# Local attention with an overlapped gated MLP: scores ahead of the feed-forward phases, and exponentials ahead of the GELUs, in the gate steps

## The reference, cut to what matters

```python
for i in range(6):
    x = attn_layer(shift_tokens(x), Wqkv[i], q_scale[i], k_scale[i], Wo[i]) + x
    x = ffn_layer(shift_tokens(x), ln_g[i], ln_b[i], W1[i], b1[i], W2[i], b2[i]) + x
# attn_layer: 16 heads of 64; q and k normalised and rotated; windows of 32 queries see
# 64 keys (their own window and the one before): softmax(8 q k + mask) v, then Wo
# ffn_layer:  layer norm, then (a + b1a) * gelu(gate + b1g) @ W2 + b2, inner width 341
```

## The kernel before, in words

| s mod 4 | phases in the step | length of a step |
|---|---|---|
| 0 | 2 | 15.7 us on the mean |
| 1 (gate step) | 3 | 21.0 us on the mean |
| 2 | 4 and 0 | 19.1 us on the mean |
| 3 | 5 and 1 | 18.6 us on the mean |

## Time and profile before

### The profile page before, as it was taken

One profiled execution on the slowest core, in us unless ns is written; L12 is line 12 of the kernel. 1 busy time (PEld: TensorE's weight loads), 2 busy tenths in 40 slices (PEclk: granted clock), 3 DMA queues, 4 the chain that ended last, 5 costly groups with the idle time before them and its releaser, 6 DMA issues. The chain is left out here.

```text
span 4666.0 us, 101858 instructions
## 1 busy us (share of the span) xinstructions
PE 3974.8 (85%) x41249; PEld 2095.7 (45%) x41249; DVE 2827.2 (61%) x5103; ACT 2272.8 (49%) x4209; POOL 1358.8 (29%) x645
## 2 busy tenths in 40 slices
PE   5666977889994997399999999999999969998888
PEld 2223433233332343166666666666666642333335
DVE  4774333676673333587777878787787746672225
ACT  2111212677772332176666666667666624652112
POOL 2441000111100000166666666566665500000000
PEclk8887978799996998699999999999999978997889
DMA  0000000666651000123232232322322200000000
GB/s 15 0 0 19 0 11 13 221 202 195 200 191 43 0 0 3 42 69 91 62 90 59 61 91 59 89 64 57 92 59 60 57 17 1 1 1 10 10 10 10
DMA packets 157210, 265.27 MB, mean 57 GB/s; under 512 B 33940, under 2 KB 69075, under 8 KB 154304
## 3 DMA queue, kind: packets, MB, share of 16 engines
q1 hardware_dynamic: 154674, 258.31, 18.8%
q10 hardware_dynamic: 2062, 0.38, 0.0%
HBM read 89.88 MB, written 68.16 MB: 34 GB/s over the span
## 5 line engine op out<-in xcount | busy, mean ns | idle before, releaser
L1987 POOL TENSOR_TENSOR b2f_norm<-b2f_norm,b2f_minus_half 128x16 f32<-128x16 f32 x192 | 554.8, 2907 | 275.8 <-DVE b2f_norm L2330 275.8
L1977 POOL TENSOR_TENSOR b2f_q<-b2f_q,b2f_q_part 128x1024 f32<-128x1024 f32 x96 | 228.0, 2375 | 951.8 <-DVE b2f_q_part L2320 951.8
L1435 ACT ACTIVATE b1a_weights<-b1a_b_ps 128x512 f32<-128x512 f32 x512 | 277.4, 597 | 41.0 <-PE b1a_b_ps L1358 39.3
L1542 DVE TENSOR_REDUCE b1a_tops<-b1a_a_ps 128x1 f32<-128x512 f32 (+3 forms) x512 | 244.6, 501 | 44.9 <-PE b1a_a_ps L1314 43.3
L1521 DVE TENSOR_REDUCE b3a_tops<-b3a_a_ps 128x1 f32<-128x512 f32 (+3 forms) x384 | 194.5, 552 | 107.2 <-PE b3a_a_ps L1314 104.4
L2329 DVE TENSOR_REDUCE b2f_norm<-xn 128x16 f32<-128x1024 f32 x192 | 234.2, 1220 | 11.9 <-ACT xn L2212 4.8
L2221 ACT ACTIVATE b2f_prob<-b2f_odd_ps,b2f_bias,b2f_norm 128x64 f32<-128x64 f32 x768 | 232.0, 446 | 10.9 <-DVE b2f_bias L2346 10.0
L2221 ACT ACTIVATE b2f_prob<-b2f_even_ps,b2f_bias,b2f_norm 128x64 f32<-128x64 f32 x768 | 231.9, 450 | 2.3 <-DVE b2f_bias L2346 2.3
L1247 POOL TENSOR_SCALAR b1a_k_op<-b1a_k_op,b1a_extra 128x1024 bf16<-128x1024 bf16 x32 | 90.6, 2843 | 485.8 <-ACT b1a_k_op L1456 485.8
L2271 ACT ACTIVATE b2f_v_rows<-b2f_q_ps 128x1024 f32<-128x1024 f32 x96 | 98.2, 1023 | 268.5 <-PE b2f_q_ps L2049 147.3
L1980 POOL TENSOR_TENSOR b2f_k<-b2f_k,b2f_k_part 128x1024 f32<-128x1024 f32 x96 | 227.5, 2370 | 0.8 <-DVE b2f_k_part L2320 0.8
(11 more groups left out here) (498 smaller groups left out, 8940.4 us busy)
## 6 DMA issues: line engine op xcount, KB each, us to landing
b2f_values<-b2f_v_rows SPq DMA_DIRECT2D x1534, 64.0 KB
position_scratch<-b1a_e_sb SPq DMA_DIRECT2D x128, 512.0 KB, 3.0
b1a_band<-position_scratch SPq DMA_DIRECT2D x128, 384.0 KB, 3.9
b2f_wqkv<-in_b2f_wqkv SPq DMA_DIRECT2D x6, 1536.0 KB, 6.5
b2f_turn<-in_c_rotary SPq DMA_DIRECT2D x6, 1024.0 KB, 8.2
b2f_wo<-in_b2f_wo SPq DMA_DIRECT2D x6, 512.0 KB, 9.4
b1f_up<-in_b1f_up SPq DMA_DIRECT2D x1, 2304.0 KB
b1f_down<-in_b1f_down SPq DMA_DIRECT2D x1, 2304.0 KB
```

What stands on the lines that cost most here:

```text
L1435: act.activation(weights[:, s % P_RING, c, lo:QW], b_room(s, c)[:, lo:QW], ACT.Exp).then_inc(S.exps_ready, 1)
L1542: ins = dve.tensor_reduce(out, src, AX_X, ALU.max)
L1977: pool.tensor_tensor(G.q[:, g % 2], G.q[:, g % 2], G.q_part[:], ALU.add) \
L1987: pool.tensor_tensor(part, part, G.minus_half[:, 0:HEADS], ALU.pow) \
```

## The change

In gate steps TensorE does the scores ahead of project_v and the phases, as in all other steps; and ScalarE does the 16 exponentials ahead of the GELUs. No wait, no buffer and no instruction of the two engines is added or removed by the source; the semaphores' waits stay inside the functions that move.

```diff
@@ tensor, step loop
-                gates = any(phase == 3 for f, phase in feed_forward(s))
-                if not gates and 0 <= s - 1 < n_tiles:
+                if 0 <= s - 1 < n_tiles:
                     scores(s - 1, here)
                 if s < n_tiles:
                     project_v(s)
                 feed(s, range(6))
-                if gates and 0 <= s - 1 < n_tiles:
-                    scores(s - 1, here)
                 if 0 <= s - 2 < n_tiles:
                     weigh_values(s - 2, other)
@@ scalar, step loop
-                ffn(s, 3)
                 if 0 <= s - 1 < n_tiles:
                     exps(s - 1, here)
+                ffn(s, 3)
                 ffn(s, 0)
```

## The result

The changed kernel takes 4741.59 us (median of 4 runs, 4739.1 to 4745.72) against 4668.3 us for the kernel before, measured beside it (4 runs). The ratio is 1.0155, with a 95% interval of 1.0134 to 1.0176: slower by 73 us. The profiled execution took 4739.1 us. Page and windows of the kernel after; the windows' columns are us, each engine's busy time, and, in rows of single windows, PEclk, DMA share and GB/s. The first sum is that of the 22 gate steps, the second that of the 22 steps behind them, as in the earlier trace rows.

A forecast was written before the change was run, and what follows sets the result against it. The prediction took gate steps to be bounded by TensorE's chain of late scores, paused weighing and next q projection. Gate steps +55 us and steps behind -5 us gave +50 us on 4672.5 us: 4722.5 us, range 4685 to 4750 us.

The forecast's parts named there:

- rival A: The forecast itself: in gate steps the GELUs' end sets the next projection, at the lower clock; +50 us, chance 0.73.
- rival D: Table load uncovered in the step behind, or a switch costs more than its load: +72 to +78 us; chance 0.12.
- The bound before: Gate steps bounded by TensorE's chain: late scores, weighing with pauses (48.6 us in all), projection of the next q.
- Rival B: TensorE is never held by the GELUs and gate steps fall to 17.97 us: -66 us, 4606 us; chance 0.07.
- What takes their place: In gate steps the next projection of q waits for all three GELUs, ending some 6.2 us later in s = 33.
- steps (1) to (5): In s = 33, chain from the probabilities' transposes through v, exponentials, table load, GELUs: projection of q starts 19.9 us in.
- The gate term: The 22 gate steps grow from 20.98 to 23.5 us each: +55 us, or +25 us with the full clock.
- (6): The projection of q behind the new wait runs at the lower clock: 3.46 us in place of 1.98 us.
- The step behind: The 22 steps behind the gate steps shorten from 19.05 to 18.8 us: -5 us, bounds 0 and -10 us.
- The sign "18.6 to 18.9 us": Expected length of each step behind a gate step in the profile after, if the forecast was right.
- The moved table load: The exponentials' table load, 1.28 us, moves into the step behind, covered there: nothing; without cover +28 us.
- Rival C: About the same: full clock through the new pause, steps behind gain 10 us; +15 us at most, 4687 us; chance 0.08.

The follow-up runs named there:

- run 1: The changed kernel with ScalarE as in the kernel before (GELUs ahead of the exponentials), so only the scores moved; 4605.05 us, ratio 0.9887.
- run 2: The kernel before with only ScalarE's exponentials moved ahead of the GELUs, scores still behind the phases; 4810.46 us, ratio 1.0339.
- run 4: The changed kernel with 8 of the 16 exponentials ahead of the GELUs and 8 behind them in gate steps; 4660.3 us, ratio 1.0012.
- run 3: The changed kernel with five extra unread matmuls behind the weighing in each gate step, keeping TensorE busy in the wait; 4687.87 us, ratio 1.007.

## Why the prediction was right, and where its size was off

The forecast was 4722.5 us (4685 to 4750) and slower; measured were 4741.59 us. The mechanism was rival A's and is shown; the size, +73 us for the +50 us forecast, was in the range only because rival D had set its upper end at 4750 us. Rival D's own number, +72 to +78 us, was the nearer one, by luck: neither of its two causes is there. Point by point:

**The bound before**, late scores and a weighing with pauses: right. Moving the scores alone brings the gate step to 17.98 us on the mean and takes the pauses from 48.6 us to 4.6 us (run 1). That it meets the 17.97 us of s = 21 to 0.01 us is luck: in run 1 single gate steps take 17.19 to 18.92 us, and s = 21 takes 17.47 us. What the pauses are the prediction had only in part: that two runs of tiny matmuls stand behind each other brings them on, but it is the arrival of TensorE's instructions that ends them (last section). Rival B's gain of 66 us is there too, less the 20 us that run 1 gives back in the steps behind.

**What takes their place**, the wait for the GELUs: right, by runs 1, 2 and 4. In s = 33 steps (1) to (5) of the working fit nearly to the digit: counted from the step's start, 19.9 us was forecast for the projection of q, and 2575.31 - 2555.40 = 19.91 us came. The forecast of 90 to 110 us for the wait met 104.7 us.

**The gate term was mis-sized**: +55 us forecast, +74.2 us measured. The step that failed is the rounding from this one gate step to all of them, 23.5 us for 24.36 us. Two things are in it. First, the projection starts 20.58 us into the step on the mean, not 20.0 us, which is some 13 us. The copy of v starts at 11.61 us on the mean where s = 33 has 10.93 us. Half of that difference is TensorE, whose project_v starts at 9.27 us on the mean for 8.91 us in s = 33; the other half is that in 12 of the 22 gate steps the copy waited still longer, for the transfers of `values`. I had looked at that wait in s = 33 alone, where it ended first. Second, (6) took 3.46 us, the value behind a pause of 4.38 us; it is 3.78 us in most steps and 3.73 us on the mean, some 6 us.

**The step behind was mis-signed**: -5 us forecast, +5.4 us measured. The gain I described exists: without the low clock these steps take 409.33 us (run 3), 9.8 us less than before and at the bound I had given. But the low clock outlasts the projection of q and slows that of k, 2.97 us in the rows above for 1.88 us at the full clock. That delays everything behind it on TensorE, which is busy for 410.81 us of these 424.47 us, 14.5 us more than in run 3. I had counted the clock once, in the gate step, and not in this one: 15.1 us. The sign "18.6 to 18.9 us" for these steps was missed too, 19.29 us, though it isn't past the 19.5 us set for rival D.

**The moved table load** was costed at nothing, and is nothing (run 3), so the first cause of rival D falls. A switch costs its load: in the rows above the GELUs follow the load's end by 0.02 us, and the load follows the last exponential by 0.02 us. The first exponential too follows its load by 0.02 us in s = 34 (2592.51 + 1.28 to 2593.81), so the 0.99 us of the earlier trace rows were the wait for the bias, and D's second cause falls as well. The estimate of 30 us more, by the drain that the Trainium skill states in "ScalarE: Activation LUTs", section "What ACT_TABLE_LOAD costs", is not borne out by this trace.

**Rival C** fell with the clock: in every gate step of the changed kernel the projection behind the wait took 3.4 us or more, while run 3, where the clock does stay up, lands at +0.7%, outside of "about the same" too.

It stays open why the transfers of `values` hold the copy of v in 12 of 22 gate steps, by up to 0.9 us beyond what project_v does, and not in the others.

## What to carry to other kernels

When an instruction is moved ahead of another on an in-order engine, look for who waits for the one that is now second. Here the exponentials were wanted early, but the GELUs held a PSUM bank that the next step's first matmul writes, so whatever is placed ahead of them delays that matmul by nearly its own time (run 4). A wait made on TensorE is to be priced with the lower clock behind it, through every matmul until the clock is back: without that clock the 80 us would be 29 us here. The waits that the old order had are to be priced in the same way, for they take their own slow matmuls with them when they go. And when a change has two halves on two engines, time each alone: one of these two is worth 1.1%, and 1.4% with the table loaded in an idle place, though the intervals of these two overlap.

## What the hardware showed that I had not expected

Extra work made a kernel faster: 110 matmuls whose results nobody reads, 59 us of TensorE's time in the gate steps, took 51 us off the changed kernel's local attention (run 3).

TensorE's pauses between two runs of 64 tiny matmuls each, 256 instructions a run as the profile counts them, are 1.8 to 2.2 us on the mean and up to 5.1 us, and they nearly go when ten larger matmul records (project_v and the gate matmuls) stand between the runs (4.6 us left in run 1). What TensorE lacks in them is its next instructions, and the traces show it in two ways.

The first is where the pauses stand. Count TensorE's instructions from the start of the trace: matmuls, weight loads, and its semaphore and drain instructions. In the eight traces kept here TensorE pauses 133 times for over 0.5 us with nothing that it waited for, and all 133 pauses stand ahead of an instruction whose number leaves 127 or 128 when divided by 256. In the kernel before, that mark moves back through the weighing by 47 of its 128 matmul records from one gate step to the next: it stands ahead of record 103 in s = 13, 56 in s = 17, 9 in s = 21 and, around the end, 90 in s = 25. The pauses there are 2.07, 2.22, 0.27 and 4.38 us. The three gate steps with the mark in the first 17 records (s = 21, 53 and 65) have the three shortest pauses, 0.2 to 0.6 us, and are the three shortest steps, 17.97 to 18.36 us. The work is the same in each; the place of the mark is not, and the step's length goes with it.

The second is a DMA queue of the kind "instruction", here on the page of the kernel before (packets, MB, share of the 16 DMA engines' span):

```profile
q8 instruction: 330, 5.41, 0.5%
```

All its packets have 16,384 bytes, and in the kernel before there are 242 of them between the first and the last rotation of local attention, as many as marks. Each of the 133 pauses of the eight traces ends 1.2 to 1.6 us after such a packet has landed. In s = 25 TensorE stops at 2407.53 us, the packet runs from 2409.62 to 2410.62 us, and TensorE goes on at 2411.91 us. The Trainium skill, "Runtime: NRT & Kernel Launch", section "Instruction fetch mechanics", says that fetching is hidden behind the issue of instructions; at these marks it is not, by the numbers above.

In the kernel before, the five gate steps in which the next layer's weights were loaded (a DMA share of 0.62 in s = 25) have the five longest pauses inside the weighing, 2.9 to 4.4 us for at most 2.3 us in the others. Why the packet comes so late, there above all, is open.
